# Row maxima negated and turned by VectorE's 32x32 block transposes instead of TensorE transposes and a ScalarE copy

## The reference

```
x = x + attention(layernorm(x))          # x: 4 batches x 512 rows x 128
q = xn @ Wq        -> 16 heads of 64, times 64 ** -0.5
k, v = split(xn @ Wkv)                    # one key head and one value head for all 16
attn = softmax(q @ k.T)                   # 512 x 512 for each of 64 (batch, head) pairs
out  = layernorm((attn @ v) @ Wo)
x = x + experts(layernorm(x))             # 8 experts, top 2 of each row
```

## Time and profile before

| | us |
|---|---|
| median of three timed runs | 621.6 (621.18 to 623.62) |
| the profiled execution, its own time | 620.37 |
| its span, first to last instruction | 618.6 |
| TensorE busy in the span | 579.3 (94%) |
| VectorE busy | 388.5 (63%) |
| GpSimd busy | 395.4 (64%) |
| ScalarE busy | 307.1 (50%) |

### The profile page before, as it was taken

How to read it: one execution, slowest core, us unless ns; L and a number is a source line. 1 busy time by engine, 2 the same in 40 slices (tenths; PEclk the granted TensorE clock), 3 DMA queues, 4 the chain that set the end, 5 groups by cost and what they waited for, 6 DMA issues and landing times. The chain is left out here.

```text
span 618.6 us, 8866 instructions
## 1 busy us (share of the span) xinstructions
PE 579.3 (94%) x2611; PEld 330.1 (53%) x2611; DVE 388.5 (63%) x792; ACT 307.1 (50%) x576; POOL 395.4 (64%) x329
## 2 busy tenths in 40 slices
PE   8799999999999998998999989999997979999990
PEld 6464555444554454454545535444443567888880
DVE  4967557656646878584567786975384468444443
ACT  2345646455546554463556445545635553455540
POOL 5457677658668855598598558959745934354331
PEclk9999999999999999798999999999999999999996
DMA  5111012010101200061000000000004400230005
GB/s 162 69 70 70 2 70 73 1 69 3 72 24 48 73 0 2 6 229 76 2 2 3 1 2 17 23 1 2 12 1 123 118 22 27 67 94 29 21 16 204
DMA packets 26990, 29.46 MB, mean 48 GB/s; under 512 B 7523, under 2 KB 18021, under 8 KB 26944
## 3 DMA queue, kind: packets, MB, share of 16 engines
q1 hardware_dynamic: 24672, 24.66, 12.3%
q0 software_dynamic: 2272, 4.24, 2.1%
HBM read 13.50 MB, written 15.32 MB: 47 GB/s over the span
## 5 line engine op out<-in xcount | busy, mean ns | idle before, releaser
L1134 ACT ACTIVATE prob<-s_ps 128x512 f32<-128x512 f32 x256 | 150.5, 598 | 177.0 <-PE s_ps L1240 175.1
L1058 DVE TENSOR_REDUCE rowmax<-max_ps 128x1 f32<-128x512 f32 x256 | 174.2, 690 | 101.4 <-PE max_ps L1209 99.1
L989 POOL TENSOR_TENSOR fold<-prob 128x1024 f32<-128x1024 f32 x63 | 149.8, 2377 | 94.5 <-ACT prob L1134 93.9
L1254 PE MATMUL pv_ps<-prob,v 128*64 128x512 f32 x512 | 139.0, 623 | 0.0
L1238 PE MATMUL s_ps<-q_hl,khh 128*128 128x512 f32 x256 | 118.5, 463 | 0.6 <-ACT prob L1134 0.6
L1209 PE MATMUL max_ps<-khh,q_hl 128*128 128x512 f32 x256 | 103.3, 409 | 7.7 <-DVE rowmax L1058 3.9
L1240 PE MATMUL s_ps<-q_hm,kly 65*128 65x512 f32 x256 | 102.3, 400 | 0.0
L1238 PEld LDWEIGHTS s_ps<-q_hl,khh 128*128 128x128 f32 x256 | 48.9, 191 | 79.5 <-ACT prob L1134 59.8
L995 POOL TENSOR_TENSOR psums<-fold 128x512 f32<-128x512 f32 x63 | 82.3, 1306 | 4.9
L1209 PEld LDWEIGHTS max_ps<-khh,q_hl 128*128 128x128 f32 x256 | 49.1, 192 | 27.3 <-DVE rowmax L1058 11.2
L1240 PEld LDWEIGHTS s_ps<-q_hm,kly 65*128 65x128 f32 x256 | 49.0, 191 | 8.9 <-issue 3.4
(11 more groups left out here) (230 smaller groups left out, 767.2 us busy)
## 6 DMA issues: line engine op xcount, KB each, us to landing
sorted_rows<-raw_w SPq DMA_DIRECT2D x36, 260.0 KB, 2.6
raw_w<-in_gate_upT SPq DMA_DIRECT2D x8, 512.0 KB, 8.3
wd<-in_downT SPq DMA_DIRECT2D x8, 256.0 KB
raw_w<-parts SPq DMA_DIRECT2D x8, 256.0 KB, 3.9
psums<-sorted_rows SPq DMA_DIRECT2D x22, 65.0 KB, 1.9
x<-in_x SPq DMA_DIRECT2D x4, 256.0 KB, 4.1
out<-x SPq DMA_DIRECT2D x4, 256.0 KB, 2.3
xs_first<-sorted_rows SPq DMA_DIRECT2D x15, 65.0 KB, 2.2
```

The costliest lines, as they stand in the source:

```text
L989: nc.gpsimd.tensor_tensor(fold[:, :, :], prob[:, head % 4, 0:2, :], prob[:, head % 4, 2:4, :], ALU.add).then_inc(prob_folded, 1)
L1058: nc.vector.tensor_reduce(rowmax[:, group % 2, it, i:i + 1], max_ps[:, k % 2, :], AX_X, ALU.max).then_inc(max_done, 1)
L1134: nc.scalar.activation(prob[:, head % 4, jt, :], s_ps[:, k % 2, :], ACT.Exp, scale=SCALE).then_inc(exp_done, 1)
L1254: last = nc.tensor.matmul(pv_ps[DH * hd:DH * hd + DH, :], v[:, b % 2, jt, :], prob[:, head % 4, jt, :], start=(jt == 0), stop=(jt == JT - 1))
```

## The change

SHIFT moves from TensorE and ScalarE to VectorE. VectorE multiplies the 16 (or 8) new columns of `rowmax` by -1 into `less_max`, a tile of 32 columns whose other columns are zero, and then transposes the four blocks of 32 partitions x 32 columns one after the other into `mrow`, which has now 32 partitions (head and tile) of 128 values. The layout of `rowmax` becomes head by head, tile by tile. The DMAs read 8 partitions of 128 values instead of 2 of 512. TensorE's step, its PSUM bank and the wait of the next user of that bank are gone, and so is the ScalarE copy.

```diff
-            rowmax = sb(att, "rowmax", [P, 2, TPB, 4])
-            mrow = sb(att, "mrow", [4, 2, S], F32R)
+            rowmax = sb(att, "rowmax", [P, 2, 4 * JT])
+            less_max = sb(att, "less_max", [P, 2, 32], F32R)
+            mrow = sb(att, "mrow", [32, 2, P], F32R)
...
+                            first = (head % 4 + h) * JT
                             sp.dma_start(q_hm[DH:DH + 1, slot:slot + 2, :].bitcast(F32),
-                                         mrow[h:h + 2, u % 2, :].bitcast(F32)).then_inc(mrow_in[u % 2], 16)
+                                         mrow[first:first + 2 * JT, u % 2, :].bitcast(F32)).then_inc(mrow_in[u % 2], 16)
...
+                link(dve, nc.vector.memset(less_max[:, :, :].bitcast(F32), 0.0))
...
+                        col = i * JT + it
                         if i == 0 and it == 0 and group >= 2:
-                            dve.wait_ge(shift_mm, group)
-                        nc.vector.tensor_reduce(rowmax[:, group % 2, it, i:i + 1], max_ps[:, k % 2, :], AX_X,
+                            dve.wait_ge(mrow_ready, group)
+                        nc.vector.tensor_reduce(rowmax[:, group % 2, col:col + 1], max_ps[:, k % 2, :], AX_X,
                                                 ALU.max).then_inc(max_done, 1)
+                    if kind == "SHIFT":
+                        head, heads = shift_heads[u]
+                        group, i = divmod(head, 4)
+                        cols = slice(i * JT, (i + heads) * JT)
+                        dve.wait_ge(max_done, (head + heads) * JT)
+                        if u >= 2:
+                            rows_came(dve, u - 2)
+                        link(dve, nc.vector.tensor_scalar(less_max[:, u % 2, cols], rowmax[:, group % 2, cols], -1.0, None,
+                                                          ALU.mult))
+                        for n in range(P // 32):
+                            part = slice(32 * n, 32 * n + 32)
+                            last = nc.vector.transpose(mrow[:, u % 2, part].bitcast(F32),
+                                                       less_max[part, u % 2, :].bitcast(F32))
+                        last.then_inc(mrow_ready, 1)
...
-                    if kind == "SHIFT":
-                        heads = shift_heads[u][1]
-                        act.wait_ge(shift_mm, u + 1)
-                        if u >= 2:
-                            rows_came(act, u - 2)
-                        nc.scalar.activation(mrow[0:heads, u % 2, :], shift_bank(u)[0:heads, :], ACT.Copy,
-                                             scale=-1.0).then_inc(mrow_ready, 1)
...
-                    if kind == "SHIFT":
-                        head, heads = shift_heads[u]
-                        pe.wait_ge(max_done, (head + heads) * JT)
-                        group, i = divmod(head, 4)
-                        for t in range(TPB):
-                            last = nc.tensor.transpose(shift_bank(u)[0:heads, t * P:(t + 1) * P],
-                                                       rowmax[:, group % 2, t, i:i + heads],
-                                                       ident[:, :])
-                        last.then_inc(shift_mm, 1)
```

More of the change, by code:

```diff
@@ L691, in bass_preln_mqa_moe_kernel @@
             x_turned xnT_sb xh_ready xl_ready k_mm kh_ready kl_ready v_mm v_ready
-            q_mm q_hi q_lo q_top max_mm max_done shift_mm mrow_ready score_mm exp_done
+            q_mm q_hi q_lo q_top max_mm max_done mrow_ready score_mm exp_done
             pv_mm raw_ready prob_folded head_sum sum_mm recip_done norm_mm ao_ready
@@ L696, in bass_preln_mqa_moe_kernel @@
          x_turned, xnT_sb, xh_ready, xl_ready, k_mm, kh_ready, kl_ready, v_mm, v_ready,
-         q_mm, q_hi, q_lo, q_top, max_mm, max_done, shift_mm, mrow_ready, score_mm, exp_done,
+         q_mm, q_hi, q_lo, q_top, max_mm, max_done, mrow_ready, score_mm, exp_done,
          pv_mm, raw_ready, prob_folded, head_sum, sum_mm, recip_done, norm_mm, ao_ready,
@@ L863, in k_bank @@
                 return pv_ps if b == 0 else q_ps
-            def shift_bank(n):
-                return sum_ps if n == 0 else q_ps
             block = att.enter_context(nc.Block())
@@ L1152, in bank_read @@
                     return {"XT": (xnT_sb, u + 1), "K": (kl_ready, u + 1), "V": (v_ready, u + 1),
-                            "Q": (q_lo, 2 * (u * UP + a + 1)), "SHIFT": (mrow_ready, u + 1)}[kind]
+                            "Q": (q_lo, 2 * (u * UP + a + 1))}[kind]
                 def keep_busy(times):
@@ L1168, in _ @@
                         keep_busy(BUSY[kind])
-                    if kind in ("XT", "K", "V", "Q", "SHIFT", "YT", "X3T", "LOGIT", "RANK") and (kind, u) not in (("K", 0), ("SHIFT", 0)):
+                    if kind in ("XT", "K", "V", "Q", "YT", "X3T", "LOGIT", "RANK") and (kind, u) != ("K", 0):
                         if in_bank:
```

## The result

The changed kernel takes 640.3 us (median of four executions, 638.1 to 641.6), the kernel before 621.4 us: ratio 1.029, 95% interval 1.025 to 1.033. Forecast were 627.5 us and a range of 616 to 633. The sign was right, the size was not.

A forecast was written before the change was run, and what follows sets the result against it. TensorE was taken to bound the attention. The profiled 620.4 us plus 4.5 for SHIFT waits net of gains and 2.2 for the clock gave 627.1, stated as 627.5 us since that execution ran below the median; range 616 to 633.

The forecast's parts named there:

- What stands in its way: At 11 of 15 SHIFTs after the start-up, VectorE's TENSOR_SCALAR waits for the end of GpSimd's running fold.
- after most SHIFTs: Expected sign in the profile: MAX matmuls wait 1.2 us on VectorE's reduction after most SHIFTs, 2.4 us twice.
- my own sum: Held SHIFTs' waits set against the gains over all SHIFTs: 2.6 + 4.2 + 0 - 1.1 - 1.2 = +4.5 us.
- What goes: TensorE's four transposes per SHIFT leave its path, 5.8 us together; ScalarE's 17 copies, 10 us, count as nothing.
- the hidden SHIFT: VectorE's SHIFT, 0.65 us if unhindered, would fit its 1.46 us of idle time after the last reduction needed.
- Rival 1: TENSOR_SCALAR gets in before the fold or is not held, so SHIFT is hidden: -3.9 us, 616.5 to 617.7 us; 20%.
- The transposes: Four 32x32 transposes per SHIFT on VectorE take 0.5 us, with 0.38 and 0.86 as the ends.
- Rival 2: VectorE's transposes are held by GpSimd's second fold too, 1.3 us at 11 SHIFTs: +14 us, 641 us; 12%.
- The clock: TensorE's two new stalls of 2.4 us may lower its granted clock: +2.2 us, with 0 and 5 as ends.
- My own sign of being wrong: Forecast is wrong if the MAX matmul waits are absent, or PEclk falls in more than two new places.
- likeliest case: Whole kernel with TENSOR_SCALAR held by folds and some clock loss: 627.5 us, own range 624 to 632; 55%.

The follow-up runs named there:

- negating kernel: Changed kernel, but VectorE's reduction itself negates into `less_max`, so the TENSOR_SCALAR is gone and the four transposes stay: 620.8 us, 0.995 of before.
- the new stalls filled: Changed kernel with matmuls of no use put into TensorE's stalls behind the SHIFTs, ahead of the waiting MAX matmuls: 636.5 us, 1.023 of before.
- negating kernel with one transpose: Negating kernel with one 128x32 transpose in place of four 32x32 at 12 SHIFTs, and four transfers per SHIFT: 623.1 us, 0.998 of before.
- the hold alone: Kernel before plus one TENSOR_SCALAR of 128x16, result unused, on VectorE at each SHIFT: 631.6 us, 1.014 of before.
- all its stalls filled: Changed kernel with unused matmuls in the stalls behind SHIFTs and also in three stalls the kernel before has: 632.5 us, 1.018 of before.
- one slot earlier: Changed kernel with SHIFT one slot earlier in the order of steps on every engine: 640.6 us, 1.027 of before.

## Why the prediction was right and where it was wrong

- **What stands in its way: right.** The TENSOR_SCALAR is held at exactly the 11 SHIFTs foreseen and at no other, until 0.03 us behind the fold's end, and removing it alone gives back some 19 us. The rule of the Trainium skill, "SBUF — State Buffer" (section "SBUF: two separate sides"), that named it agrees with these rows. The waits are longer than the 1.2 and 2.4 us that I gave, 1.40 and 2.72, and "after most SHIFTs" was too much even by my own sum: three waits are of 1.40 us, three of 0.54 and two of 2.72.
- **What goes, and the hidden SHIFT: right.** Rival 1 gave -3.9 us for a SHIFT without a hold; the negating kernel has that SHIFT, and the interval of its ratio is -0.7 to -5.4 us. Its stall where the statistics follow was expected from that rival at 0.65 us and is 0.94.
- **The transposes: mis-sized.** I took 0.5 us for four, between 0.38 and 0.86; they take 0.84. At eight SHIFTs that is +2.7 us, which brings the sum of 4.5 to 7.2 us, against +8.1 of full-clock time. The stalls of 1.40 and 0.77 us show that the length counts in full there. I had argued from the number of columns, 32 against the 128 of BN_STATS; but four BN_STATS take 0.86 us and four transposes 0.84, so the columns did not count here.
- **Rival 2: its mechanism was wrong, its 641 us right by accident.** The transposes ran beside GpSimd's second fold in 0.84 us. The rule that I cited for it is in the Trainium skill, "VectorE: DVE Perf Modes" (section "What auto-detection actually checks"). Its condition of a single source and a destination in SBUF is met by these transposes, and they were not held; the rest of the rule leaves room for that in what firmware enables, which no run here shows. The 641 us were luck: they came from 1.3 us at 11 SHIFTs that nobody waited, and what stood in their place was the clock.
- **The clock: the step that failed.** I gave +2.2 us with 5 as the upper end; it is +8.9. What I said of the new stalls was not the mistake: no low stretch follows one of 1.40 us in either profile of the changed kernel, and behind the two of 2.72 us stand 3.4 us in the first profile and 3.4 and 6.8 us in the second, 1.7 and 5.1 us of loss. The mistake is that I let the old stalls keep the price that they had in one trace. I took the one of 1.48 us in the earlier trace rows for a stall that leaves the clock alone. In the changed kernel that very stall, 0.14 us longer, was followed by 10.2 us at half the clock, which is 5.1 us of loss. The same 10.2 us follow it with the new stalls filled (1.54 us) and in the negating kernel with one transpose, which has no new wait of over 0.28 us near it (1.13 us). Of the 8.6 us by which the loss of the two first profiles differs, 5.1 us are this stretch, 1.7 the one at 216 and 1.7 the one at 540, for which the forecast had no term. My own sign of being wrong came too: the clock fell at three new places in the first profile and at four in the second.
- **What stays open.** Over several executions the loss goes with the waits: 14.2 us without the held instruction, 18.1 with the hold alone, 23.3 in the changed kernel, 13.1 with all its stalls filled. But with only the new stalls filled it is 21.1, and nine of 72 executions of the kernel before have as much with no new stall at all. A stall's size does not say what it does: behind the old one near 250 us (1.2 to 1.7 us of wait) the profiles here have 0, 3.4, 6.8 or 10.2 us of low clock. What decides that is not shown.
- **The range** of the likeliest case, 624 to 632, summed the ends of its own terms too low: 2.9 us for the transposes and 2.8 us for the clock on top of 627.5 are 633.2. With both as measured, 7.2 + 8.9 us from 622.3, it is 638.4. With the loss of single executions of the unchanged kernel spread over 12 us, an upper end of 5 us for the clock was not one.

## What to carry to other kernels

Before a small instruction is moved to VectorE, ask what it will find on GpSimd at that very moment: a 0.16 us operation of the held kind costs the rest of GpSimd's instruction, and all that is queued behind it. When it is moved out of the way, ask the same of its neighbours. Often the work can be had without such an instruction, here by the negation within the reduction, which reads PSUM, or by ScalarE. Where an edit makes TensorE wait, price the clock with the loss of several executions, not with one stall that went well in one trace, and count the old stalls in.

## What the runs showed of the hardware

- A transpose of four 32x32 blocks in one 128x32 instruction takes 0.20 us, as long as one block of 32x32 does; four instructions take 0.84.
- A TENSOR_REDUCE from PSUM with the negation takes 0.69 us for 128x512, no more than without.
- Beside GpSimd's fold a TENSOR_SCALAR of 128x16 takes up to 2.29 us and not 0.16, and a TENSOR_TENSOR of 128x256 with two sources in SBUF 2.07 us and not 0.42 (one slot earlier). 32x32 transposes, TENSOR_REDUCE and BN_STATS take their usual time.
- A transfer into `q_hm` on SyncE's queue lasts 0.63 us in the median with 8 pieces and 1 KB in all, 0.66 us with 8 pieces and 4 KB (the negating kernel), and 0.59 us with 2 pieces and 4 KB (the kernel before). Four times the bytes cost 0.03 us. Eight transfers per SHIFT in place of two made EXP matmuls wait 15.6 us in all.
- Low stretches of the clock between two stretches of work last 3.4, 6.8 or 10.2 us here. The same program has executions with a loss of 11 and of 22 us, which is most of the spread of the kernel before, 620.0 to 629.6 us.
